# Final attention of a transformer block on one Trainium2 core: the scores of two heads alternate between the two row halves of the array, the steps go by pairs of heads, and the quantiser's lower bound is taken in bf16

## What is computed

```
for each of 16 sequences x (256 x 512), ctx (256 x 512):
    # two attentions with 16 heads of 32 channels; q, k, v and the probabilities are quantised to 8 bits
    x = attn(ln1(x), ln1(x)) + x              # sim = fq(q) fq(k)^T; out = fq(softmax(sim)) fq(v)
    x = attn(ln2(x), ctx) + x
    fq(t) = (clip(round(t / delta) + 128, 0, 255) - 128) * delta
    # feed forward, 2048 wide, gated with an exact GELU
    a, g = split(ln3(x) @ ff_w1 + ff_b1)
    x = (a * gelu(g)) @ ff_w2 + ff_b2 + x
    # final attention: 8 heads of 64 channels, 256 queries, 256 keys, float32, not quantised
    q = ln(x) @ Wq + bq; k = ln(ctx) @ Wk + bk; v = ln(ctx) @ Wv + bv
    out = x + softmax(q k^T / 8) v
```

## Time and profile before

| | |
|---|---|
| profiled execution | 3276.47 us, of it 3274.7 us span |
| median of three runs | 3278.27 us |
| TensorE busy | 2937.3 us (90% of the span) |
| VectorE busy | 1924.1 us (59%) |
| ScalarE busy | 1612.9 us (49%) |
| GpSimd busy | 807.4 us (25%) |
| mean granted TensorE clock | 0.955 of full speed |

### The profile page before, as it was taken

One profiled execution on the slowest core, in us unless ns is written; L12 is line 12 of the kernel. 1 busy time (PEld: TensorE's weight loads), 2 busy tenths in 40 slices (PEclk: granted clock), 3 DMA queues, 4 the chain that ended last, 5 costly groups with the idle time before them and its releaser, 6 DMA issues. The chain is left out here.

```text
span 3274.7 us, 54866 instructions
## 1 busy us (share of the span) xinstructions
PE 2937.3 (90%) x18304; PEld 2336.9 (71%) x18304; DVE 1924.1 (59%) x4469; ACT 1612.9 (49%) x3866; POOL 807.4 (25%) x1179
## 2 busy tenths in 40 slices
PE   3688888888888886599999997999999999999998
PEld 2455566555555553389999996888888888888886
DVE  5699999999999997543333335333333333333332
ACT  3466666666666665321111112555555555555552
POOL 1233333333333332133333322111111111111110
PEclk8799999999999997699999998999999999999997
DMA  5233333333333333230100104000000000000000
GB/s 145 42 68 73 73 78 76 74 74 74 72 75 77 73 74 62 67 113 26 38 26 26 38 19 129 27 26 26 26 26 26 26 26 26 26 26 26 32 14 13
DMA packets 328217, 168.59 MB, mean 51 GB/s; under 512 B 276960, under 2 KB 293344, under 8 KB 328160
## 3 DMA queue, kind: packets, MB, share of 16 engines
q1 hardware_dynamic: 328160, 167.87, 20.2%
HBM read 75.54 MB, written 25.17 MB: 31 GB/s over the span
## 5 line engine op out<-in xcount | busy, mean ns | idle before, releaser
L584 ACT ACTIVATE e<-S,bias,qk_scale 128x256 f32<-128x256 f32 x1024 | 563.5, 562 | 153.4 <-DVE pq L691 149.0
L683 DVE TENSOR_SCALAR e<-e,rsum 128x256 f32<-128x256 f32 x1024 | 337.1, 391 | 2.9
L669 DVE TENSOR_REDUCE negmax<-S 128x4 f32<-128x1024 f32 x256 | 310.9, 1215 | 21.9 <-PE S L493 19.3
L1543 POOL TENSOR_TENSOR mid_partsB<-mid_actB,mid_partsB 128x256 fp32r<-128x256 f32 x128 | 94.2, 736 | 679.3 <-DVE mid_partsB L1449 679.3
L554 ACT ACTIVATE shifted<-PJ,round_col,inv 128x512 f32<-128x512 f32 x192 | 149.2, 777 | 215.0 <-PE PJ L162 212.8
L153 PE MATMUL PJ<-w_a_wo,oT 128*128 128x512 f32 x512 | 243.5, 620 | 2.6 <-ACT oT L593 1.8
L162 PE MATMUL PJ<-hT,w_a_wq 128*128 128x256 f32 x1536 | 204.4, 291 | 24.3 <-DVE w_a_wq L414 19.9
L760 POOL TENSOR_TENSOR bias<-negmax,qk_scale 128x4 f32<-128x4 f32 x256 | 72.5, 283 | 596.8 <-DVE negmax L669 595.9
L162 PEld LDWEIGHTS PJ<-hT,w_a_wq 128*128 128x128 f32 x1536 | 192.1, 195 | 37.4 <-issue 37.4
L1350 ACT ACT_TABLE_LOAD x121 | 155.2, 1283 | 126.5 <-PE AG1B L162 75.4
L514 PE MATMUL O<-pT,vQ 128*32 128x256 bf16 x1024 | 110.4, 297 | 110.5 <-DMA pT<-pq 57.6
(11 more groups left out here) (174 smaller groups left out, 5834.0 us busy)
## 6 DMA issues: line engine op xcount, KB each, us to landing
x_in<-in_x_dram SPq DMA_DIRECT2D x16, 512.0 KB, 3.6
ctx_in<-in_ctx_dram SPq DMA_DIRECT2D x16, 512.0 KB, 3.7
mid_dram<-x SPq DMA_DIRECT2D x16, 512.0 KB, 2.7
y_inA<-mid_dram SPq DMA_DIRECT2D x16, 512.0 KB, 3.5
part_dram<-x3A SPq DMA_DIRECT2D x16, 512.0 KB, 3.6
y_inB<-mid_dram SPq DMA_DIRECT2D x16, 512.0 KB, 3.3
kv_in<-in_ctx_dram SPq DMA_DIRECT2D x16, 512.0 KB, 4.6
baseB<-part_dram SPq DMA_DIRECT2D x16, 512.0 KB, 3.2
```

The costliest lines, as they stand in the source:

```text
L584: nc.scalar.activation(e[:, s, i, :], S[s][:, i // 2, i % 2, :], ACT.Exp, bias=bias[:, s, i:i + 1], scale=qk_scale[:, ph.a:ph.a + 1], accu ...
L669: nc.vector.tensor_reduce(negmax[:, g % 2, :], S[g % 2][:].rearrange("p i q n -> p (i q) n"), AX_X, ALU.max, negate=True).then_inc(max_don ...
L683: nc.vector.tensor_scalar(e[:, s, i, :], e[:, s, i, :], rsum[:, s, i:i + 1], WMAX, ALU.mult, ALU.min).then_inc(prob_scaled, 1)
L1543: nc.gpsimd.tensor_tensor(mid_parts[:, f % 2, 1, :], mid_act[:, f % 2, :], mid_parts[:, f % 2, 0, :], ALU.subtract).then_inc(mid_low_done, 1)
```

## The change

In the final attention the unit of a step becomes a pair of heads. `pe_scores4` computes both heads of pair p, head 2p into bank XT0 and head 2p + 1 into bank XT1, and alternates between them product by product, so that one product uses rows 0 to 63 and the next rows 64 to 127. Even steps f issue the scores of pair f/2 and the value products of the pair before; odd steps issue the transposes of the pair, which go back into the bank that the head's scores stood in. The maxima, exponentials and copies follow by pairs. The scores of a pair wait for the copies of the pair before. In the quantiser, the first VectorE operation subtracts ROUND and takes the upper bound, and writes bf16 (whole numbers up to 127; below -256 they may be rounded, which the lower bound takes away); the second takes the lower bound from bf16 to bf16. ScalarE's `act_shift` waits for the first of the two operations instead of the second.

```diff
+            rounded = sb(one, "rounded", [P, 2, D], BF16)
...
-                    act.wait_ge(quantised, n - 1)
+                    act.wait_ge(clipped, n - 1)
...
-                nc.vector.tensor_scalar(shifted[:, bank, :], shifted[:, bank, :], ROUND + QMAX, ROUND + QMIN,
-                                        ALU.min, ALU.max).then_inc(clipped, 1)
+                nc.vector.tensor_scalar(rounded[:, bank, :], shifted[:, bank, :], ROUND, QMAX,
+                                        ALU.subtract, ALU.min).then_inc(clipped, 1)
...
-                nc.vector.tensor_scalar(dst, shifted[:, bank, :], ROUND, None, ALU.subtract).then_inc(quantised, 1)
+                nc.vector.tensor_scalar(dst, rounded[:, bank, :], QMIN, None, ALU.max).then_inc(quantised, 1)
...
-                S4, T4 = (bank[:].rearrange("p (t n) -> p t n", t=TT) for bank in XT)
+                X4 = [bank[:].rearrange("p (t n) -> p t n", t=TT) for bank in XT]
...
-                def pe_scores4(pe, b, h):
+                def pe_scores4(pe, b, p):
...
-                        pe.wait_ge(exp4_done, TT * n)
-                    r = DH1 * (h % 2)
+                        pe.wait_ge(p4T_done, H1 * b + 2 * p)
                     for qt in range(TT):
-                        ins = nc.tensor.matmul(S4[:, qt, :], q4T[r:r + DH1, h // 2, qt * P:(qt + 1) * P],
-                                               k4T[r:r + DH1, h // 2, :], start=True, stop=True)
-                    ins.then_inc(scores4_done, 1)
+                        for i in range(2):
+                            r = DH1 * i
+                            ins = nc.tensor.matmul(X4[i][:, qt, :], q4T[r:r + DH1, p, qt * P:(qt + 1) * P],
+                                                   k4T[r:r + DH1, p, :], start=True, stop=True)
+                            if qt == TT - 1:
+                                ins.then_inc(scores4_done, 1)
...
                     pe.wait_ge(exp4_done, TT * (n + 1))
-                    if h >= 1:
-                        pe.wait_ge(p4T_done, n)
...
                         pe_up(pe, b, f)
-                        if attend:
-                            pe_scores4(pe, b - 1, f)
-                            if f >= 1:
-                                pe_transpose4(pe, b - 1, f - 1)
+                        if attend and f % 2 == 0:
+                            pe_scores4(pe, b - 1, f // 2)
+                        if attend and f % 2 == 1:
+                            for h in (f - 1, f):
+                                pe_transpose4(pe, b - 1, h)
                         if f >= 2:
                             pe_down(pe, b, f - 2)
-                        if attend and f >= 2:
-                            pe_pv4(pe, b - 1, f - 2)
+                        if attend and f >= 2 and f % 2 == 0:
+                            for h in (f - 2, f - 1):
+                                pe_pv4(pe, b - 1, h)
...
                         act_gate(act, b, f)
-                        if attend:
-                            if f >= 1:
-                                act_p4T(act, b - 1, f - 1)
-                            act_exp4(act, b - 1, f)
+                        if attend and f % 2 == 0:
+                            for h in (f, f + 1):
+                                act_exp4(act, b - 1, h)
+                        if attend and f % 2 == 1:
+                            for h in (f - 1, f):
+                                act_p4T(act, b - 1, h)
...
+                        if attend and f % 2 == 0:
+                            for h in (f, f + 1):
+                                dve_max4(dve, b - 1, h)
                         dve_gated(dve, b, f)
-                        if attend:
-                            dve_max4(dve, b - 1, f)
```

More of the change, by code:

```diff
@@ L1215, in pe_down @@
                     ins.then_inc(down_done, 1)
-                def pe_scores4(pe, b, h):
-                    n = H1 * b + h
-                    if h == 0:
+                def pe_scores4(pe, b, p):
+                    if p == 0:
                         for j in range(2):
@@ L1234, in pe_transpose4 @@
                     pe.wait_ge(exp4_done, TT * (n + 1))
[L1235 to L1236 removed]
                     for qt in range(TT):
                         for kc in range(TT):
[L1239 removed]
+                            ins = nc.tensor.transpose(X4[h % 2][:, kc, qt * P:(qt + 1) * P],
                                                       e4[:, h % 2, qt, kc * P:(kc + 1) * P], ident[:])
@@ L1265, in pe_sequence2 @@
                         pe_up(pe, b, f)
-                        if attend:
-                            pe_scores4(pe, b - 1, f)
-                            if f >= 1:
-                                pe_transpose4(pe, b - 1, f - 1)
+                        if attend and f % 2 == 0:
[3 more added lines that the diff above has]
+                                pe_transpose4(pe, b - 1, h)
                         if f >= 2:
                             pe_down(pe, b, f - 2)
-                        if attend and f >= 2:
-                            pe_pv4(pe, b - 1, f - 2)
-                    if attend:
-                        pe_pv4(pe, b - 1, H1 - 2)
+                        if attend and f >= 2 and f % 2 == 0:
+                            for h in (f - 2, f - 1):
+                                pe_pv4(pe, b - 1, h)
                     pe_down(pe, b, HC - 2)
                     if attend:
-                        pe_transpose4(pe, b - 1, H1 - 1)
+                        for h in (H1 - 2, H1 - 1):
+                            pe_pv4(pe, b - 1, h)
                     if attends:
-                        pe_turn(pe, b, "cT", 0)
-                        if attend:
-                            pe_pv4(pe, b - 1, H1 - 1)
-                        pe_turn(pe, b, "cT", 1)
+                        for j in range(2):
+                            pe_turn(pe, b, "cT", j)
                     pe_down(pe, b, HC - 1)
@@ L1355, in act_exp4 @@
                     for qt in range(TT):
-                        nc.scalar.activation(e4[:, h % 2, qt, :], S4[:, qt, :], ACT.Exp,
+                        nc.scalar.activation(e4[:, h % 2, qt, :], X4[h % 2][:, qt, :], ACT.Exp,
                                              bias=negmax4[:, h % 2, qt:qt + 1],
@@ L1363, in act_p4T @@
                         act.wait_ge(pv4_done, H1 * b + h - 1)
-                    nc.scalar.copy(p4T[:, h % 2], T4).then_inc(p4T_done, 1)
+                    nc.scalar.copy(p4T[:, h % 2], X4[h % 2]).then_inc(p4T_done, 1)
                 def act_sequence2(act, b, attend=attends, last=False):
@@ L1454, in dve_max4 @@
                     dve.wait_ge(scores4_done, H1 * b + h + 1)
-                    nc.vector.tensor_reduce(negmax4[:, h % 2, :], S4, AX_X, ALU.max, negate=True).then_inc(
+                    nc.vector.tensor_reduce(negmax4[:, h % 2, :], X4[h % 2], AX_X, ALU.max, negate=True).then_inc(
                         max4_done, 1)
@@ L1682, in _ @@
                         if attends:
-                            for h in range(H1 + 1):
-                                if h < H1:
+                            for p in range(H1 // 2):
+                                for h in (2 * p, 2 * p + 1):
                                     act_exp4(act, B - 1, h)
-                                if h:
-                                    act_p4T(act, B - 1, h - 1)
+                                for h in (2 * p, 2 * p + 1):
+                                    act_p4T(act, B - 1, h)
                     @block.tensor
@@ L1699, in _ @@
                         if attends:
[L1700 to L1706, removed]
+                            for p in range(H1 // 2):
+                                pe_scores4(pe, B - 1, p)
+                                for h in (2 * p, 2 * p + 1):
+                                    pe_transpose4(pe, B - 1, h)
+                                if p:
+                                    for h in (2 * p - 2, 2 * p - 1):
+                                        pe_pv4(pe, B - 1, h)
+                            for h in (H1 - 2, H1 - 1):
+                                pe_pv4(pe, B - 1, h)
             for half in range(2):
```

4 lines of the change are left out of this document (removed).

## The result

The changed kernel takes 3186.22 us (median of four runs, 3184.13 to 3188.65) against 3279.99 for the kernel before in the same comparison: a ratio of 0.971, 95% interval 0.970 to 0.973. The prediction was 3188, of a range of 3172 to 3244. The sum came out within 2 us, but its terms did not: the loop of half B gave 80 us where 69 stood, everything ahead of it (stage 1, where the quantiser is, and half A) gave 11 where 17 stood, and the tail 1 where 3 stood.

What follows compares the result with a forecast made beforehand. Stage 1 was taken as bound by VectorE, half B by TensorE. From the profiled 3276.5 us, less 69 (scores), 17 (quantising) and 3 (tail), came 3187.5, given as 3188 us; range 3172 to 3244.

Steps and rivals of the forecast that it cites:

- Scores: one block of 1.15 us instead of 2.30: Final attention, half B: float32 scores of both heads run at once on two row halves, saving 1.15 us a pair.
- the rule of program order: TensorE, from the Trainium skill: matmuls start and end strictly in program order; by it a pair's scores need five slots.
- 60 pairs, 69 us: Half B's loop: 15 sequences with four pairs each, 60 x 1.15 = 69 us less.
- No new wait: Half B's loop: the new order makes TensorE wait nowhere, with 0.5 us to spare at the second head's transposes; cost nothing.
- Quantising: 20.7 us of VectorE, 17 on the path: Stage 1: 180 fills save VectorE 0.115 us each, 20.7 us; five sixths shorten the time, 17 us less.
- The tail, 3 us: Last 46 us, TensorE at 1.2 GHz: a pair goes from 9.3 to 9.1 us; taken as 3 us less.
- (a): Half B's scores: only neighbouring matmuls overlap, five slots; a pair saves 0.93 us, 56 in all: 3200 us; chance 0.20.
- (b): Half B's scores: float32 row halves don't run at once; a pair saves 0.29 us, 17 in all: 3242 us; chance 0.20.
- (c): Half B: longer way from scores to copies stops TensorE once or twice a sequence, 30 us back: 3218 us; chance 0.08.
- (d): Half B: a wait at the first pair's transposes lowers the clock inside sequences, up to 180 us, kernel slower; chance 0.03.
- quantising at its worst bound: Stage 1: the second VectorE operation gets no faster and the first costs 0.02 us more, 4 us more over 180 fills.
- full overlap: Half B's scores: a pair's eight records take four slots of 0.216 us; own range 3174 to 3206 us; chance 0.47.

Runs made afterwards that it cites:

- head-by-head kernel: The changed kernel with the loops around a pair's products swapped, so that each head's four records stand together (a a b b): 3185.46 us, ratio 0.971.

## Why the prediction was right, step by step

- *Scores: one block of 1.15 us instead of 2.30.* Right, and shown: 12.44 us for a pair of steps where 12.4 was given, 1.06 us for the block, and 1.92 with both heads on one half. Taking the bf16 scores of stage 1 as the model for float32 was sound, and so was putting that row above the rule of program order; the head-by-head kernel fits with the bf16 products' overlap, which are written in that order too.
- *60 pairs, 69 us.* The term was mis-sized: 80 us. At 1.14 us each, 60 pairs give 68. The other 12 are 0.8 us a sequence outside the steady pairs; I followed a sequence only for new waits, not for old ones that the new order takes away. Most of TensorE's idle time in the loop, 1172.9 - 1166.2 = 6.8 us, is such waits, and it was in the trace before.
- *No new wait.* Right: 1.0 us of idle time in the whole loop. That ScalarE's table loads are worth nothing because nobody waits for it was not quite so: TensorE waited for ScalarE twice a sequence. Those waits are gone; how much of that is due to the table loads is open.
- *Quantising: 20.7 us of VectorE, 17 on the path.* The second operation's size was right (280 ns given, 280 to 284 measured). The first costs no 0.02 us more (its median is 397 ns in both kernels, where near 415 was given), but other operations of VectorE took about as much back: by the prediction the thirteen rounds' 156 fills give VectorE 17.9 us, and they gave 17.3. The step that failed is the share: five sixths of it on the path, taken from VectorE's 94% busy time. Measured were six tenths, 10.3 of 17.3 us, and a round got 0.79 us shorter, not 1.4. The 94% is a mean over groups, and by the reading above the gain fell on the groups in which TensorE is the longer one.
- *The tail, 3 us.* 1 us. I left out that the copy waits for the value products two heads back. Nor do the prediction's own pair costs (9.3 and 9.1 us) give 3: four pairs of them give 0.8.
- *Rivals.* (a) and (b) are refuted by the block of 1.06 us; (b)'s own size, 0.29 us a pair, was right when built. (c) and (d) didn't occur.

The errors of + 11, - 6 and - 2 nearly cancelled, and the remaining 3 us were met by the base: the sum starts from 3276.5, and the kernel before has a median of 3279.99 in this comparison. The saving was forecast as 89 us and is 94 between the medians. That the total came out within 2 us is luck and no evidence for the single terms. One sum in the prediction is off: with quantising at its worst bound full overlap ends at 3276.5 - 69 - 3 + 4 = 3208 or 3209 us, not 3206, which changes nothing.

## What to carry to other kernels

Matmuls of 64 channels, float32 too, ran at the same time here when they used different row halves and different banks and stood in one block (one bank for both wasn't tried); put the two heads' products together, and both orders tried within the block cost the same. Before multiplying a saved time by the busy share of its engine, compare the engines group by group: a stage that is "94% VectorE" can be bound by TensorE exactly where the saving lies. And a kernel with work left out can bring a lower clock with it, so read its clock before comparing. And where an engine is nearly always busy, its few idle microseconds show what a new order may give besides: here 6 us of the 80. A wait of TensorE in a stage called "VectorE's" was worth even more, 16 us for a spare PSUM bank.

## What the runs showed of the hardware

- Two row halves run float32 matmuls at once: eight records in two banks hold TensorE for 1.06 us, against 1.92 on one half. One head's four records alone took 1.06 too.
- Records of different row halves don't keep program order among each other: with four records of one half written first, the other half's first record starts 0.02 us after the first.
- A single-source VectorE operation on 128x512 takes 281 ns with bf16 in and out. With float32 in, the median is 397 ns for the first operation, with float32 out in one kernel and with bf16 out in the other, and 417 for the old second one with bf16 out. The narrow output alone brings nothing; narrow input with narrow output does.
- GpSimd's small `dsum` operation took 583 ns on average with the old quantiser and 395 with the new one (392 in the kernel that has the quantiser's edit alone). Which part of that edit does it, no run separates.
- In the tail with the value products moved, TensorE's longest idle gap is 0.68 us once the clock has fallen to 1.2 GHz, and the granted clock stays at 0.50 to the end. Before it fell, TensorE had waited 1.06 us for the queries and 1.80 and 0.25 us for exponentials, and it fell during a wait of 0.68 us for a copy.
- In stage 1 with half the output projection and the new quantiser the granted clock was 0.52 or 0.53 for the 7 us behind TensorE's wait of 2.06 us, in 7 of 13 rounds; 12 records of 512 columns took 5.41 us there instead of 2.94.
